# Two attention layers in a six-layer kernel: last half of the heads in chunk order 3, 0, 2, 1, and the next layer's normalisations in six pieces

## The reference

```
x = x + 0.5 * L0_ffn(norm(x))      expert layer: 8 experts, argmax router, gelu, inner norm
x = x + L0_attn(norm(x))           attention: 16 heads of 8, causal softmax, then @ wo + bo
x = x + 0.5 * L0_ffn(norm(x))      expert layer again
x = x + 0.5 * L1_ffn(norm(x))      ternary weights, relu
x = x + L1_attn(norm(x))           attention, biased q, k, v, no output projection
x = x + 0.5 * L1_ffn(norm(x))      ternary layer again
norm(x) = (x - mean) / sqrt(var + 1e-5)   over the 128 columns of a row
softmax(q k^T / sqrt(8)) v                per head, over all keys up to the query's row
```

## Time and profile before

| | |
|---|---|
| median of 3 runs | 1215.2 us (1214.64 to 1215.71) |
| profiled execution | 1215.68 us, span 1213.9 us |
| busy: TensorE, VectorE, ScalarE, GpSimd | 90%, 83%, 55%, 5% |
| granted TensorE clock, mean | 0.975 |
| first attention, last eight turns | 572.7 to 592.2 us |
| second attention, last half without chunk 3 | 1080.5 to 1179.7 us |

### The profile page before, as it was taken

One profiled execution on the slowest core, in us unless ns is written; L12 is line 12 of the kernel. 1 busy time (PEld: TensorE's weight loads), 2 busy tenths in 40 slices (PEclk: granted clock), 3 DMA queues, 4 the chain that ended last, 5 costly groups with the idle time before them and its releaser, 6 DMA issues.

```text
span 1213.9 us, 34232 instructions
## 1 busy us (share of the span) xinstructions
PE 1091.9 (90%) x14757; PEld 492.3 (41%) x14757; DVE 1006.6 (83%) x2343; ACT 664.6 (55%) x861; POOL 65.8 (5%) x62
## 2 busy tenths in 40 slices
PE   1898976999999999999699987689999999999988
PEld 1455552333333333334345555433333333333436
DVE  8977568999999999886547657799999999998764
ACT  0322222556777777777332214145667777887773
POOL 5111001000000000000100100100000000000000
PEclk9999988999999999999799998899999999999999
DMA  5100034100000000000000000620000000000001
GB/s 158 36 1 1 1 98 117 33 3 2 2 3 2 3 2 3 3 2 3 1 1 2 1 1 1 181 64 3 2 3 2 2 2 2 3 2 3 4 3 35
DMA packets 23555, 24.07 MB, mean 20 GB/s; under 512 B 3134, under 2 KB 21220, under 8 KB 23404
## 3 DMA queue, kind: packets, MB, share of 16 engines
q1 hardware_dynamic: 22252, 18.73, 5.4%
q0 software_dynamic: 1152, 3.15, 1.0%
HBM read 13.20 MB, written 8.39 MB: 18 GB/s over the span
## 4 chain that ended last, share of the span: by engine, by line
PE 55%; DVE 37%; issue 4%; ACT 3%; DMA 1%; SPq 0%; DVEq 0%; ACTq 0%
DVE part_max L1356 25%; PE psum L1215 12%; PE psum L1237 11%; PE psum L443 10%; PE psum L1186 6%; PE psum L467 3%; ACT hidden L1319 2%; PE psum L1201 2%; PE psum L899 2%; PE psum L1243 1%; DVE xn L168 1%; PE psum L1264 1%; DVE norm_v L151 1%; PE psum L914 1%; PE psum L428 1%
## 5 line engine op out<-in xcount | busy, mean ns | idle before, releaser
L1356 DVE TENSOR_REDUCE part_max<-psum 128x1 f32<-128x512 f32 (+3 forms) x1120 | 677.1, 668 | 52.7 <-PE psum L1243 35.3
L1319 ACT ACTIVATE hidden<-psum 128x1024 f32<-128x1024 f32 (+3 forms) x640 | 539.0, 895 | 220.8 <-PE psum L1186 219.7
L1237 PE MATMUL psum<-k_slots,q_slots 128*32 128x512 f16 (+3 forms) x5120 | 389.9, 355 | 31.4 <-DVE part_max L1356 13.5
L1215 PE MATMUL psum<-hidden,v_aug 128*9 128x512 f32 (+3 forms) x2560 | 290.3, 530 | 0.1
L1237 PEld LDWEIGHTS psum<-k_slots,q_slots 128*32 128x32 f16 x5120 | 123.3, 95 | 286.2 <-DVE part_max L1356 193.1
L443 PE MATMUL psum<-parts,w_parts 128*128 128x512 f16 x768 | 179.5, 385 | 1.9 <-DVE parts L839 1.9
L1186 PE MATMUL psum<-q_slots,k_slots 32*128 32x512 f16 (+3 forms) x1472 | 141.3, 328 | 9.6 <-ACT hidden L1319 7.7
L443 PEld LDWEIGHTS psum<-parts,w_parts 128*128 128x128 f16 x768 | 73.6, 99 | 82.4 <-issue 5.7
L587 ACT CAST parts<-psum 128x512 f16<-128x512 f32 x64 | 37.2, 588 | 107.1 <-PE psum L428 107.1
L1243 PE MATMUL psum<-ident_bf,later_keys 128*32 128x128 bf16 (+2 forms) x1408 | 91.5, 250 | 0.0
L1186 PEld LDWEIGHTS psum<-q_slots,k_slots 32*128 32x128 f16 x1472 | 42.0, 91 | 99.7 <-ACT hidden L1319 49.0
(11 more groups left out here) (168 smaller groups left out, 731.4 us busy)
## 6 DMA issues: line engine op xcount, KB each, us to landing
q_slots<-q_rows SPq DMA_DIRECT2D x8, 512.0 KB, 3.8
k_slots<-k_rows POOLq DMA_DIRECT2D x24, 128.0 KB, 4.2
q_rows<-parts SPq DMA_DIRECT2D x18, 128.0 KB, 3.0
k_rows<-parts SPq DMA_DIRECT2D x18, 128.0 KB, 2.8
q_slots<-in_L_ffn_W_dram SPq DMA_DIRECT2D x2, 1024.0 KB, 6.5
k_slots<-k_rows SPq DMA_DIRECT2D x8, 128.0 KB, 4.0
q_slots<-nm_parts SPq DMA_DIRECT2D x64, 4.0 KB
out_dram<-x_res SPq DMA_DIRECT2D x4, 256.0 KB, 2.3
```

Of the source, the lines that this page charges most:

```text
L1215: last = pe.matmul(psum[VW * h:VW * h + DH + 1, O_BANK, off:CH], v_aug[:, j, G * g + h, :], probs[:, (2 * n + h // 2) % NP, h % 2, off:CH] ...
L1237: last = pe.matmul(psum[rows32(m), bank, a * w:(a + 1) * w], q_slots[:, g, qb * P + m * SLOT:qb * P + (m + 1) * SLOT], k_slots[:, G * g + ...
L1319: act.activation(probs[:, tile % NP, :, off:CH], psum[:, bank:bank + 2, off:CH], ACT.Exp, scale=scale).then_inc(exp_done, 1)
L1356: dve.tensor_reduce(part_max[:, step_no[s] % 2, h0:h0 + heads, i, kc], psum[:, bank, 0:heads * w].rearrange("p (a k) -> p a k", a=heads), ...
```

## The change

The order of chunks in the last half of the heads becomes 3, 0, 2, 1 (`LAST_CHUNKS`), and so does the order of chunks in the second expert layer and the last layer, and of the normalisations that these and the first ternary layer take. An attention layer now makes three of the next layer's normalisations (3, 0, 2) instead of two, and the next layer makes one (chunk 1). Each is cut into six pieces: statistics, then their aggregation with the seed, two Newton rounds, one round, and twice two blocks of the application. Piece p of a chunk stands at the end of the turn p + 1 turns after the chunk's output (p + 3 turns in the first attention, after its projection). By the numbers of `units_beside_quads`, chunk 3's pieces stand in turns 118 to 123, chunk 0's in 126 to 131 and chunk 2's in 150 to 155 of the second attention, and two turns later in the first. Chunk 0's quads stand in turns 116 to 123. The last unit stands in turn 152 (155 before), and in turns 116 to 123 there are 21 units.

```diff
@@ -145,7 +145,7 @@
                 own(dve.bn_aggr(s.mean_var[:, b, :], s.stats[:, b, :]))
             own.wait()
 
-        def norm_rstd(dve, own, s, eps, b0, n):
+        def rstd_seed(dve, own, s, eps, b0, n):
 
             v, r, t = s.v[:, b0:b0 + n], s.rstd[:, b0:b0 + n], s.tmp[:, b0:b0 + n]
             own(dve.tensor_scalar(v, s.mean_var[:, b0:b0 + n, 1], eps, None, ALU.add))
@@ -154,8 +154,11 @@
             own.wait()
             own(dve.tensor_scalar(r.bitcast(I32), t.bitcast(I32), -1.0, float(0x5F3759DF), ALU.mult, ALU.add))
             own.wait()
-            for _ in range(3):
-
+
+        def rstd_refine(dve, own, s, b0, n, times):
+
+            v, r, t = s.v[:, b0:b0 + n], s.rstd[:, b0:b0 + n], s.tmp[:, b0:b0 + n]
+            for _ in range(times):
                 own(dve.scalar_tensor_tensor(out=t, in0=r, scalar=-0.5, in1=r, op0=ALU.mult, op1=ALU.mult))
                 own.wait()
                 own(dve.tensor_tensor(t, t, v, ALU.mult))
@@ -163,6 +166,10 @@
                 own(dve.scalar_tensor_tensor(out=r, in0=t, scalar=1.5, in1=r, op0=ALU.add, op1=ALU.mult))
                 own.wait()
 
+        def norm_rstd(dve, own, s, eps, b0, n):
+            rstd_seed(dve, own, s, eps, b0, n)
+            rstd_refine(dve, own, s, b0, n, 3)
+
         def norm_apply(dve, s, dst, src, b):
 
             return dve.tensor_scalar(dst[:, b, :], src[:, b, :], s.mean_var[:, b, 0:1], s.rstd[:, b:b + 1],
@@ -186,6 +193,25 @@
                 norm_rstd(dve, own, scratch, 1e-5, chunk * BPC, BPC)
                 for b in range(chunk * BPC, (chunk + 1) * BPC):
                     norm_apply(dve, scratch, xn, x_res, b).then_inc(self.ready, 1)
+
+            PIECES = 6
+
+            def make_piece(self, dve, own, scratch, chunk, piece):
+                b0 = chunk * BPC
+                own.wait()
+                if piece == 0:
+                    for b in range(b0, b0 + BPC):
+                        own(dve.bn_stats(scratch.stats[:, b, :], x_res[:, b, :]))
+                elif piece == 1:
+                    for b in range(b0, b0 + BPC):
+                        own(dve.bn_aggr(scratch.mean_var[:, b, :], scratch.stats[:, b, :]))
+                    own.wait()
+                    rstd_seed(dve, own, scratch, 1e-5, b0, BPC)
+                elif piece <= 3:
+                    rstd_refine(dve, own, scratch, b0, BPC, 4 - piece)
+                else:
+                    for b in range(b0 + 2 * (piece - 4), b0 + 2 * (piece - 3)):
+                        norm_apply(dve, scratch, xn, x_res, b).then_inc(self.ready, 1)
 
 
         class Projection:
@@ -1004,8 +1030,9 @@
 
 
         HALF = NG // 2
+        LAST_CHUNKS = (3, 0, 2, 1)
         STEPS = [(g, c) for c in range(NCH) for g in range(HALF)] + \
-                [(g, c) for c in reversed(range(NCH)) for g in range(HALF, NG)]
+                [(g, c) for c in LAST_CHUNKS for g in range(HALF, NG)]
         AHEAD = 2
         SLACK = 3
         UNIT_FIXED, QUAD_FIXED = 100, 500
@@ -1132,7 +1159,6 @@
 
 
 
-            idle = max(turn for turn, (_, turn_max, _, _) in enumerate(PLAN) if turn_max)
             tail, norm_turn = {}, {}
             for turn, (_, _, _, turn_out) in enumerate(PLAN):
                 for g, c in turn_out:
@@ -1141,7 +1167,9 @@
                             tail.setdefault(turn + 1, []).append(("turned", c))
                             tail.setdefault(turn + 2, []).append(("project", c))
                         if c in next_norms.order[:next_given]:
-                            norm_turn[idle + 1 + 3 * (NCH - 1 - c)] = c
+                            summed = turn + 2 if projected else turn
+                            for piece in range(Norms.PIECES):
+                                norm_turn[summed + 1 + piece] = c, piece
 
 
 
@@ -1392,8 +1420,6 @@
                             if g == NG - 1 and not projected:
                                 rows = slice(c * BPC, (c + 1) * BPC)
                                 own(dve.tensor_tensor(x_res[:, rows, :], ctx[:, rows, :], x_res[:, rows, :], ALU.add))
-                    if turn in norm_turn:
-                        next_norms.make(dve, own, s1, norm_turn[turn])
                     for s in m_now:
                         k = step_no[s]
                         dve.wait_ge(ring_read, last_unit[s] + 1)
@@ -1402,6 +1428,8 @@
                         dve.tensor_reduce(neg_max[:, k % 2, :],
                                           part_max[:, k % 2, :, :, 0:s[1] + 1].rearrange("p h i c -> p (h i) c"),
                                           axis=AX.X, op=ALU.max, negate=True).then_inc(negmax_ready, 1)
+                    if turn in norm_turn:
+                        next_norms.make_piece(dve, own, s1, *norm_turn[turn])
 
             @blk.gpsimd
             def _(pool):
@@ -1451,17 +1479,17 @@
 
 
 
-        UP, DOWN = (0, 1, 2, 3), (3, 2, 1, 0)
-        BETWEEN, TURNING = (3, 2, 0, 1), (0, 3, 1, 2)
-        orders = (UP, UP, BETWEEN, TURNING, TURNING, DOWN)
-        norms = [Norms(f"xn_ready{i}", order) for i, order in enumerate((UP, UP, BETWEEN, BETWEEN, TURNING, DOWN))]
+        UP, TURNING = (0, 1, 2, 3), (0, 3, 1, 2)
+        orders = (UP, UP, LAST_CHUNKS, TURNING, TURNING, LAST_CHUNKS)
+        norms = [Norms(f"xn_ready{i}", order)
+                 for i, order in enumerate((UP, UP, LAST_CHUNKS, LAST_CHUNKS, TURNING, LAST_CHUNKS))]
         projections = {1: Projection(w_qkv0, False, norms[1], orders[1]), 4: Projection(w_qkv1, True, norms[4], orders[4])}
         released = expert_layer(True, orders[0], 0, norms[0], norms[1], following=projections[1])
-        released = attention_layer(projections[1], 0, True, 3, norms[2], 2, released)
-        released = expert_layer(False, orders[2], 2, norms[2], norms[3], released)
+        released = attention_layer(projections[1], 0, True, 3, norms[2], 3, released)
+        released = expert_layer(False, orders[2], 3, norms[2], norms[3], released)
         released = ternary_layer(False, orders[3], 3, norms[3], norms[4], released, projections[4])
-        released = attention_layer(projections[4], 1, False, 3, norms[5], 2, released)
-        ternary_layer(True, orders[5], 2, norms[5], None, released)
+        released = attention_layer(projections[4], 1, False, 3, norms[5], 3, released)
+        ternary_layer(True, orders[5], 3, norms[5], None, released)
 
 
 # ---- launch: one core; inputs and outputs as the reference has them ----
```

## The result

The changed kernel took 1221.46 us (median of 7 runs, 1220.34 to 1226.00), the kernel before 1215.63 us in the same comparison (7 runs). The ratio is 1.0058, with a 95% interval of 1.0046 to 1.0071: slower by 5.8 us, where +6.0 was predicted. The runs lie in two bands, 1220.3 to 1221.5 us at a granted clock of 0.976 and 1225.8 to 1226.0 us at 0.967; the profiled execution is of the upper one: 1225.84 us, span 1224.0 us, 10.2 us more than the profiled one before.

A forecast was written before the change was run, and what follows sets the result against it. It took TensorE as the bound, VectorE close behind, short of room beside the pieces. Order 0, second attention +6.3, first -0.3, layers behind 0 gave +6.0 us: 1221.2 us on the median 1215.2, range 1214.8 to 1225.5.

The forecast's parts named there:

- part 1: Last half of both attentions: new order of chunks alone, moved work moves its own time; 0 us, bounds -1 and +1.
- part 2: Second attention, turns 118 to 123: chunk 3's normalisation beside chunk 0's short quads costs 3.1 us, bounds 1.0 and 4.7.
- part 3: Second attention, turns 126 to 131: chunk 0's normalisation in a chunk 2 step costs 2.7 us, bounds 1.0 and 4.7.
- part 4: Second attention, turns 150 to 155: chunk 2's normalisation, nearly covered, costs 0.5 us, bounds 0 and 1.
- part 5: First attention: chunk 3's and chunk 0's pieces together 4.5 us, old stall gone 4.8 us; net -0.3, bounds -4 and +5.
- the stall: First attention's end before: chunk 1's output and projection queue behind chunk 3's normalisation on VectorE; its going saves 4.8 us.
- part 6: Layers behind the attentions: each loses one normalisation at its start; 0 us, bounds -1 and 0.
- A: Last halves: pieces slip into VectorE's gaps, middle normalisations hidden, stall gone, -4.8 us: 1210.4 us; chance 0.12.
- B: Last halves: four normalisations cost 1.2 us each, 4.8 in all, cancelling the stall's 4.8: 1215.2 us; chance 0.13.
- C: Matmul-bound turns: stalls of 2 us or more bring half-speed clock, up to 1.7 us each for two: 1224.7 us; chance 0.15.
- The expert layer's wait: Second expert layer: only the last normalisation shows, 0.54 us before its transposes, and that one stays.
- the (3,3) step: Chunk 3's second step in the last half: the order alone changing it by over 1 us would show the forecast wrong.

The follow-up runs named there:

- pieces late: Changed kernel, order 3, 0, 2, 1 kept, with all eighteen pieces two a turn in turns 153 to 161, behind the last unit: 1217.30 us, ratio 1.0003.
- no Newton rounds: Changed kernel with the two Newton-round pieces (2 and 3) left empty, nine of a normalisation's 24 instructions missing: 1222.05 us, ratio 1.0030.
- spaced: Changed kernel with chunk 3's pieces in every second turn 124 to 134, chunk 0's 136 to 146, chunk 2's in 153 to 155: 1217.31 us.
- old order with pieces: Kernel before, order 3, 2, 1, 0, its two normalisations cut into six pieces each in turns 156 to 162: 1210.94 us, ratio 0.9965.
- extra matmuls: Unread score matmuls added in turns without units: on the changed kernel 1224.87 us; on the kernel before with its two normalisations in pieces 1214.54 us.

## Why the prediction was right, and where it was not

The total was right, +6.0 against +5.8 in the medians, and so was the main mechanism, VectorE short of room where the pieces stand. That the figures lie so close is luck: one term was missed, and others were too large by as much.

| term | predicted | measured by steps |
|---|---|---|
| part 1, the order alone | 0 (-1 to +1) | +3.0 (2.4 and 0.6), 1.3 of it clock |
| part 2, chunk 3's, second attention | +3.1 | +2.4 |
| part 3, chunk 0's, second attention | +2.7 | +2.0 |
| part 4, chunk 2's | +0.5 | 0 |
| part 5, chunk 3's, first attention | +2.3 | +2.2 |
| part 5, chunk 0's, first attention | +2.2 | +1.6 |
| part 5, the stall goes | -4.8 | -4.2 |
| part 6, the layers behind | 0 | work 0, clock 0 to +3.3 |
| sum | +6.0 | +7.0, without the clock outside |

(The halves themselves give 6.8; the steps are rounded.)

**Part 1 failed.** "Busy 97% on either side, so moved work moves its own time" took TensorE as the bound in all places that give and take. The place that takes had 11.98 busy of 13.70 us (87%) in the prediction's own, and the place that gives, chunk 1's two steps before, had 95 and 94%:

```profile
1132.80:1149.90 17.10, 16.23 (x315) 6.84 (x311) 12.78 (x24) 13.24 (x18) 0.00 (x0) 1.00 0.01 2
1149.90:1166.00 16.10, 15.07 (x305) 6.60 (x298) 9.59 (x19) 13.20 (x17) 0.00 (x0) 1.00 0.02 4
```

Against the windows of pieces late above, the second attention gives this account, TensorE's busy time first and the time of the steps behind it. Chunk 3's two steps: +2.3 and +2.0 us. Chunk 0's two: +4.3 and +3.3. Chunk 2's two: -0.9 and -1.2. Chunk 1's two: -5.2 and -3.6. So moved work moved its own time in chunk 3's and chunk 2's steps, and took less than its own in chunk 0's; what failed is the giving side, where 5.2 us of TensorE's work left and only 3.6 us of time came back. In the last step, without units, a full quad is ScalarE's, 13.2 us busy of 14.1, and TensorE idles 15%; in the old order the turns without units were the short quads. Over the whole half it is +0.6 us of busy time and +0.6 of time.

In chunk 3's steps it wasn't VectorE that set the time, or not it alone. Its maxima there, before and changed:

```profile
L1356 DVE TENSOR_REDUCE part_max<-psum 128x1 f32<-128x512 f32 (+3 forms) x111 | 67.9, 674 | 3.6 <-PE psum L1237 1.7 <-PE psum L1243 1.3
```

```profile
L1384 DVE TENSOR_REDUCE part_max<-psum 128x1 f32<-128x512 f32 (+3 forms) x114 | 68.8, 663 | 3.7 <-PE psum L1271 1.8 <-PE psum L1265 0.8
```

Three more maxima would be 1.8 us at 0.606 each, but these are busy only 0.9 us more. In the first of the two steps VectorE's busy time didn't rise at all (35.78 and 35.70 us) while the step grew by 0.9 us and TensorE's busy time by 0.9; TensorE is busy 99% of both, VectorE 94 and 95%. The first attention's 2.4 us hold 1.3 of the clock, by the two windows above. Which part of the other 1.1 + 0.6 comes from which step's bound I read from these rows and didn't test apart.

**Parts 2, 3 and 5, the pieces.** The reckoning by VectorE's work against the room of the same turns was right in kind and in order, and high in the sum by 0.7 + 0.7 + 0.5 + 0.1 + 0.6 = 2.6 us (parts 2, 3, 4 and the two of part 5), which nearly balances the 3.0 of part 1. That the pieces are the cause is shown by taking them away (pieces late) and by making them shorter (no Newton rounds); that it is room on VectorE, by the spaced version, with the limit named there. A whole normalisation shows the other end: stops of 3.9 to 4.3 us, against my upper bound of 4.7, and the clock on top, which that bound left out. Why the reckoning was high isn't shown; it counted next to nothing of the room in the turns behind the six, into which lateness can run off.

**Part 5, the stall.** 4.2 of 4.8, inside its bounds of 4.0 and 5.8, and shown by a kernel that does nothing else.

**Part 6, the layers behind.** 0 was right for the work: the versions without Newton rounds and spaced, with the same three normalisations given, took 206.6 and 206.2 us between and 34.3 and 34.1 behind, against 206.8 and 34.1 before. The clock of these layers, 3.3 us in the profile, was in no term.

**The rivals.** A (the pieces slip into gaps) was wrong for these places, but its ground is true for others: the old order with pieces is this rival, -4.7 us. The Trainium skill's advice to break up instructions ("Perfetto Trace Analysis", Optimizing Scalar/DVE Operations) is borne out twice, with 4.2 us at the stall and 21 us in the halves against whole normalisations among the maxima. Its condition, an engine that isn't saturated, held for VectorE over the span (82%) and not in the steps that took the pieces (95%); giving them turns with room was worth another 5.5 us by the steps. B needed 1.2 us each for the four; they cost about 2.0 each, and the order came on top. C is open in part. The clock stayed at 1.00 from turn 116 to 150, so it didn't come as put; but a half-speed stretch stayed in the first attention, and the layers around lost 3.3 us to the clock in the profiled execution. Its mechanism is real, though: with whole normalisations each stop of 3.9 to 4.3 us was followed by half-speed clock amid the busy turns. The pieces kept TensorE's stops at 1.3 us or less. In the lower band (1220.3 to 1221.5) the total stands 4.7 to 5.8 us above the median before, no more than the halves' 6.8; in the upper one the clock's part comes on top. That these bands are the clock outside the two halves is likely from the steps, which never moved, and from the 1.6 us ahead of the first attention, but no profile of the changed kernel's lower band shows it.

**What would show it.** Chunk 0's second step and chunk 2's first took 1.9 + 2.5 us more than with the pieces late, and TensorE's wait for maxima was 11.3 us there: as forecast. VectorE was 95 and 94.5% busy in them, a little under the "above 95%". The wait for maxima over the last half grew from 19.4 to 28.6 us, by about as much as forecast, but not from "a few us". The expert layer's wait was 0.51. "No longer a wait above 1 us" at the first attention's end failed: 1.53 us of ScalarE was left, at half clock. "The expert layer and the last layer keep their length within 1 us" failed, by the clock (1.2 us between the attentions, 2.1 behind). And one sign of being wrong came true: the order alone made the (3,3) step 1.2 us longer in both attentions (36.0 to 37.2), where over 1 us was to count against the forecast. It pointed at part 1, and rightly.

## What to carry to other kernels

Ahead of moving small work on an engine, write beside each turn how much of that engine is left there, not in the step or the span: the same eighteen pieces cost 8.2 us by the steps in consecutive turns, and 2.7 us with twelve of them in every second turn and six behind the last unit. If a stall comes from one long piece, cut it where it stands before changing the order around it (that alone gave 4.7 us here). And a change of order isn't free because the sum of work is the same: ask at each place that gives and at each that takes which engine ends the turn. Here 5.2 us of TensorE's work left two steps, and 3.6 us of time came back.

## What was not expected of the hardware

- The clock is worth as much as the change. With the same layers between the attentions, versions with at most 30.7 us at half speed there took 206.0 to 207.0 us, and those with 40.9 or 44.3 us took 208.0 to 208.4. Behind them, without extra matmuls, 3.4 us at half speed at the last layer's start went with 34.0 to 34.3 us and 10.2 with 36.2 to 36.3. Runs of one kernel lay 1.6 to 7.5 us apart (1210.60 to 1212.22 and 1211.61 to 1219.08).
- With whole normalisations, four stops of TensorE of 3.9 to 4.3 us each were followed by 3.4 or 6.8 us of half-speed clock in its busiest stretch; with pieces there was none, at stops up to 1.3 us.
- Where such a stretch falls hangs on little. In the last step of an attention, at full quads without units, it costs 0.9 to 1.4 us (15.1 to 15.6 against 14.2 us), and it came and went with changes of a few us in other places.
- Small VectorE instructions on 128 x 4 elements took 0.16 us and followed each other at 0.196 us, so nine of them in a chain hold the engine 1.8 us, as long as three maxima over 512 columns.
